# Recommendation tower on one core: embedding features in groups of four instead of three, with both ends of the kernel reordered

## The reference

```python
e = jnp.stack([tbl_0[ids[:, 0]], ..., tbl_26[ids[:, 26]]], axis=1)      # (2048, 27, 128)
inter = einsum('bfd,bgd->bfg', e, e)[:, upper triangle without diagonal]   # 351 pairs
h = concatenate([e.reshape(B, -1), inter, dense_ctx], axis=1)              # dense_ctx: 16 columns
h = maximum(h @ W_top1 + b_top1, 0)    # W_top1 (3823, 512)
h = maximum(h @ W_top2 + b_top2, 0)    # W_top2 (512, 256)
y = h @ W_top3                         # (256, 1)
```

## Time and profile before

| what | before |
|---|---|
| median of 3 runs | 555.32 us (553.8 to 556.41) |
| the profiled execution's own time | 555.27 us |
| its span | 553.3 us |
| mean granted TensorE clock | 0.994 |
| busy: PE, PEld, DVE, ACT, POOL | 515.7, 422.9, 246.4, 256.3, 399.0 us |
| matmuls, gathers | 4337, 411 |

### The profile page before, as it was taken

How to read it: one execution, slowest core, us unless ns; L and a number is a source line. 1 busy time by engine, 2 the same in 40 slices (tenths; PEclk the granted TensorE clock), 3 DMA queues, 4 the chain that set the end, 5 groups by cost and what they waited for, 6 DMA issues and landing times.

```text
span 553.3 us, 12824 instructions
## 1 busy us (share of the span) xinstructions
PE 515.7 (93%) x4337; PEld 422.9 (76%) x4337; DVE 246.4 (45%) x501; ACT 256.3 (46%) x504; POOL 399.0 (72%) x415
## 2 busy tenths in 40 slices
PE   0677999999899999999999998999999999999996
PEld 0556888878688787888788787888878887788884
DVE  3564543535254343635335352443436353362544
ACT  3664545363354545345453533545353453533542
POOL 6777777777777777777777777777777777777700
PEclk9988999999999999999999999999999999999999
DMA  8885222222222222222221222222222222222200
GB/s 178 258 271 171 55 66 55 54 56 55 65 56 51 58 56 65 52 55 55 66 58 50 55 54 64 56 50 56 55 63 53 54 54 64 53 50 54 53 11 2
DMA packets 26553, 38.82 MB, mean 70 GB/s; under 512 B 12510, under 2 KB 16078, under 8 KB 26488
## 3 DMA queue, kind: packets, MB, share of 16 engines
q0 software_dynamic: 13152, 26.96, 18.9%
q1 hardware_dynamic: 10410, 9.95, 6.2%
q10 hardware_dynamic: 2926, 1.09, 0.8%
HBM read 37.96 MB, written 0.01 MB: 69 GB/s over the span
## 4 chain that ended last, share of the span: by engine, by line
PE 61%; POOL 21%; issue 8%; DMA 7%; DVE 2%; ACT 1%; DVEq 0%; ACTq 0%
POOL gathered L331 21%; PE p_hid L712 14%; PE p_hid L714 13%; PE p_hid L713 13%; PE p_prod L784 9%; PE p_group L682 7%; DMA gathered<-tbl_dram,idx 4%; DMA w_stage<-tbl_dram 1%; PE p_group L669 1%; PE p_group L670 1%; PE p_hid_t L749 1%; DVE w_low L495 1%; DMA w_stage<-w_dense_dram 1%; PE p_group L699 1%; ACT emb L380 0%
## 5 line engine op out<-in xcount | busy, mean ns | idle before, releaser
L331 POOL DMA_INDIRECT gathered<-tbl_dram,idx x411 | 398.8, 970 | 127.3 <-issue 119.5
L712 PE MATMUL p_hid<-w_high,emb_high 128*128 128x512 f32 x424 | 180.6, 426 | 0.0
L714 PE MATMUL p_hid<-w_high,emb_low 128*128 128x512 f32 x424 | 168.0, 396 | 0.0
L713 PE MATMUL p_hid<-w_low,emb_high 128*128 128x512 f32 x424 | 166.8, 393 | 0.0
L510 DVE TENSOR_TENSOR emb_low<-p_group,emb_high 128x384 fp32r<-128x384 f32 x144 | 79.1, 549 | 155.9 <-ACT emb L380 155.4
L365 ACT ACTIVATE emb_high<-p_group 128x384 fp32r<-128x384 f32 x144 | 69.9, 485 | 156.2 <-PE p_group L682 139.1
L380 ACT ACTIVATE emb<-p_group 128x384 f32<-128x384 f32 x144 | 124.0, 862 | 0.0
L682 PE MATMUL p_group<-identity,gathered 128*128 128x128 f32 x411 | 72.9, 284 | 29.0 <-DMA gathered<-tbl_dram,idx 28.9
L714 PEld LDWEIGHTS p_hid<-w_high,emb_low 128*128 128x128 f32 x424 | 80.3, 189 | 19.0
L713 PEld LDWEIGHTS p_hid<-w_low,emb_high 128*128 128x128 f32 x424 | 81.1, 191 | 12.6
L712 PEld LDWEIGHTS p_hid<-w_high,emb_high 128*128 128x128 f32 x424 | 81.0, 191 | 12.2
(11 more groups left out here) (86 smaller groups left out, 364.4 us busy)
## 6 DMA issues: line engine op xcount, KB each, us to landing
fetched<-tbl_dram SPq DMA_DIRECT2D x640, 0.5 KB
w_stage<-w_dense_dram SPq DMA_DIRECT2D x27, 256.0 KB, 3.7
gathered<-tbl_dram,idx POOLq DMA_INDIRECT x411
pick_ids<-ids_rows_dram ACTq DMA_DIRECT2D x7, 125.0 KB
w_stage<-w_pairs_dram SPq DMA_DIRECT2D x3, 252.0 KB
w_stage<-w_dram SPq DMA_DIRECT2D x2, 256.0 KB, 4.5
w_stage<-tbl_dram SPq DMA_DIRECT2D x2, 250.0 KB
ctx_sb<-ctx_rows_dram ACTq DMA_DIRECT2D x14, 13.5 KB, 1.8
```

What stands on the lines that cost most here:

```text
L331: pool.indirect_dma_start(gathered[:, slot, k, :], None, tables[f], bass.IndirectOffsetOnAxis(ap=idx[:, t, f:f + 1], axis=0),).then_inc(gr ...
L712: nc.tensor.matmul(dst, high, w_high, start=start, stop=False)
L713: nc.tensor.matmul(dst, high, w_low, start=False, stop=False)
L714: return nc.tensor.matmul(dst, low, w_high, start=False, stop=stop)
```

## The change

1. **Groups of four.** `FEATS = 4`: six groups of four features and one of three in place of nine of three. The order of a tile becomes `[0, 1, 2, 3, 4, 5, "pairs", 6]`, with the rest of the work at the same step numbers; the picks are made at steps 2 and 3.
2. **Rings.** The ring holds 4 groups, 16 gathers; `emb_low` holds two groups in place of three, so `group_low` waits for layer 1 of two groups before.
3. **Start.** SP issues the remaining weights right after the first five, the table of row numbers and the first pick's ids; the ids of tiles 1 to 15 (now laid out so that each partition reads one piece of 1,620 bytes) come after weight piece 8, the context of all tiles (one DMA of 16 columns, in place of one of 27 per tile) after piece 22, the biases and `w3` behind all weights. In tile 0, layer 1 of a group goes ahead of the transposes.
4. **End.** In the last tile, `relu1` and `hid1_to_low` of tile 14 come behind the last group's copies; the four rounds of pair products come behind layer 1 of group 5 and `transpose_hid1`; the bias of the last layer 2 is put in by a matmul (`last_bias2`) in place of DVE's addition.
5. `hid1` shares its memory with `products`; two waits guard it.

```diff
-    FEATS = 3
-    GROUPS = NF // FEATS
-    RING = 6
+    FEATS = 4
+    GROUPS = -(-NF // FEATS)
+    LAST_FEATS = NF - FEATS * (GROUPS - 1)
+    RING = 4
     SPLIT = 3
+    SPLIT_LOW = 2
...
-    SEQUENCE = [0, 1, 2, 3, 4, 5, 6, "pairs", 7, 8]
-    LAST_SEQUENCE = [0, 1, 2, 3, 4, "pairs", 5, 6, 7, 8]
+    SEQUENCE = [0, 1, 2, 3, 4, 5, "pairs", 6]
+    LAST_SEQUENCE = [0, 1, 2, 3, 4, "pairs", 5, 6]
+    PICK_STEPS = [2, 3]
...
+    def feats_of(g):
+        return range(FEATS if g < GROUPS - 1 else LAST_FEATS)
...
-            sp.dma_start(idx[:, 1:TILES, :], ids_t[:, 1:TILES, :]).then_inc(ids_loaded[1], 16)
+            sp.dma_start(table_row_sb[:], table_row).then_inc(table_row_loaded, 16)
+            sp.dma_start(pick_ids_first[:], picked_t[0].partition_broadcast(PICK_ROWS)).then_inc(pick_ids_loaded, 16)
+            for n in range(STAGES, len(STAGED)):
+                load_weight(n)
+                if n == 8:
+                    sp.dma_start(idx[:, 1:TILES, :], ids[:, 1:TILES, :]).then_inc(ids_loaded[1], 16)
+                if n == 22:
+                    sp.dma_start(ctx_sb[:], ctx_rows).then_inc(ctx_loaded, 16)
...
-                    if (ahead_t, ahead) == (LAST, GROUPS - 2):
-                        relu1(LAST - 1)
...
+                if n == GROUPS - 2 and t == LAST:
+                    relu1(LAST - 1)
...
+                wait(dve, group_used, s - SPLIT_LOW + 1)
-                nc.vector.tensor_tensor(emb_low[:, s % SPLIT, 0:n, :], bank_of(t, g)[:, 0:n, :],
+                nc.vector.tensor_tensor(emb_low[:, s % SPLIT_LOW, 0:n, :], bank_of(t, g)[:, 0:n, :],
...
+                wait(dve, hid1_low_done, t)
...
-                nc.vector.tensor_tensor(hid2[:], p_hid2[:, 0:HID2], b2_rows[:], ALU.add).then_inc(bias2_done, 1)
-                dve.wait_ge(bias2_done, t + 1)
-                nc.vector.scalar_tensor_tensor(out=hid2[:], in0=hid2[:], scalar=0.0, in1=w3_rows[:],
+                summed = p_hid2[:, 0:HID2] if t == LAST else hid2[:]
+                if t < LAST:
+                    nc.vector.tensor_tensor(hid2[:], p_hid2[:, 0:HID2], b2_rows[:], ALU.add).then_inc(bias2_done, 1)
+                    dve.wait_ge(bias2_done, t + 1)
+                nc.vector.scalar_tensor_tensor(out=hid2[:], in0=summed, scalar=0.0, in1=w3_rows[:],
...
+            def last_bias2(t):
+                pe.wait_ge(bias2_done, t)
+                nc.tensor.matmul(p_hid2[:, 0:HID2], identity[:], b2_rows[:], start=True, stop=False)
...
+                    if t == 0:
+                        layer1_group(t, n)
                     ahead_t, ahead = ORDER[ORDER.index((t, n)) + 2]
...
-                    else:
+                    elif t > 0:
                         layer1_group(t, n)
...
                 transpose_group(t, 6)
                 layer1_group(t, 5)
                 transpose_hid1(t - 1)
-                transpose_group(t, 7)
-                layer1_group(t, 6)
-                transpose_group(t, 8)
                 for r in range(ROUNDS):
                     pair_products(t, r)
                 layer2(t - 1)
-                layer1_group(t, 7)
-                layer1_group(t, 8, [0])
+                layer1_group(t, 6, [0])
                 last_transpose_pairs(t, [0])
-                layer1_group(t, 8, [1, 2])
+                layer1_group(t, 6, [1, 2])
                 last_transpose_pairs(t, [1, 2])
                 layer1_pairs(t, by_chunk=True)
+                last_bias2(t)
                 last_transpose_hid1(t)
```

More of the change, by code:

```diff
@@ L35, in dlrm_tower @@
     HID2 = w2.shape[1]
-    TILES = B // P
-    CTX = ctx_rows.shape[1]
-    assert D == P and B % P == 0 and TILES % 2 == 0 and TILES >= 6 and NF == 27
+    CTX = ctx_rows.shape[2]
+    assert ids.shape[0] == P and D == P and TILES % 2 == 0 and TILES >= 6 and NF == 27
     assert HID1 == 512 and HID2 <= 512 and HID1 % P == 0
@@ L42, in dlrm_tower @@
     ROWS_I = NF // 3
-    assert CTX == NF
+    assert CTX <= NF
     ROW = DELTAS + 1
@@ L83, in gathered_feats @@
             return range(FEATS)
-        return [k for k in range(FEATS) if g * FEATS + k != PICKED
+        return [k for k in range(LAST_FEATS) if g * FEATS + k != PICKED
                 and not (g * FEATS + k == FETCHED and t in FETCH_TILES)]
-    ids_t = ids.rearrange("(t p) f -> p t f", p=P)
-    ctx_t = ctx_rows.rearrange("(t p) n -> p t n", p=P)
     out_t = out.rearrange("(t p) o -> t (p o)", p=P)
@@ L140, in dlrm_tower @@
         prod = sb("prod", [P, NF, ROWS_Q])
+        with nc.sbuf_tensor("hid1", [P, HID1], F32) as hid1:
+            pass
         products = sb("products", [P, WIDE, ROWS_Q])
@@ L164, in dlrm_tower @@
         group_gathered = [sem(f"group_gathered_{k}") for k in range(RING)]
-        ctx_loaded = [sem(f"ctx_loaded_{k}") for k in range(2)]
+        ctx_loaded = sem("ctx_loaded")
         pick_ids_loaded = sem("pick_ids_loaded")
@@ L308, in _ @@
             sp.dma_start(w3_rows[:], w3.partition_broadcast(P)).then_inc(consts_loaded, 16)
-            for n in range(STAGES, len(STAGED)):
-                load_weight(n)
             sp.wait_ge(fetch_ids_loaded, 16)
@@ L384, in group_copies @@
                 if t == 0:
-                    for n in range(staged_upto(FEATS * g), staged_upto(FEATS * (g + 1))):
+                    for n in range(staged_upto(FEATS * g), staged_upto(FEATS * g + len(feats_of(g)))):
                         weight_high(n)
@@ L410, in last_place_ctx @@
                 act.wait_ge(pairs_transposed, t)
-                act.wait_ge(ctx_loaded[t % 2], (t // 2 + 1) * 16)
-                nc.scalar.activation(pairs[:, :, DELTAS], ctx_sb[:, t % 2, :], ACT.Copy).then_inc(last_placed, 1)
+                act.wait_ge(ctx_loaded, 16)
+                nc.scalar.activation(pairs[:, 0:CTX, DELTAS], ctx_sb[:, t, :], ACT.Copy).then_inc(last_placed, 1)
             def last_place_pairs(t):
@@ L461, in _ @@
                         group_copies(ahead_t, ahead)
-                if n == 0 and t == 0:
+                if n == 0 and t == 2:
                     act.wait_ge(consts_loaded, CONSTS * 16)
@@ L614, in _ @@
                     ahead_t, ahead = ORDER[k + 2]
-                    if (ahead_t, ahead) == (LAST, GROUPS - 3):
+                    if (ahead_t, ahead) == (LAST, GROUPS - 1):
                         copy_hid1(LAST - 1)
-                    if (ahead_t, ahead) == (LAST, GROUPS - 1):
-                        hid1_to_low(LAST - 1)
                     if ahead == "pairs":
@@ L628, in _ @@
                     hid1_to_low(t - 2)
+                if n == GROUPS - 2 and t == LAST:
+                    hid1_to_low(LAST - 1)
                 if n == 4 and t >= 2:
                     layer3(t - 2)
-                if n in (4, 5) and picks_start(t):
-                    make_pick(t, n - 4)
+                if n in PICK_STEPS and picks_start(t):
+                    make_pick(t, PICK_STEPS.index(n))
                 if n == "pairs" and t < LAST:
@@ L685, in transpose_group @@
                     pe.wait_ge(rows_fetched[n % 2], (n // 2 + 1) * P * 16)
-                    last = nc.tensor.transpose(bank_of(t, g)[:, FETCHED % FEATS, :], fetched[:, n % 2, :], identity[:])
+                    last = nc.tensor.transpose(bank_of(t, g)[:, FETCHED - g * FEATS, :], fetched[:, n % 2, :], identity[:])
                 last.then_inc(group_transposed, 1)
```

58 lines of the change are left out of this document (29 added, 29 removed).

## The result

The changed kernel takes 556.52 us (median of 13 runs, 555.71 to 557.7), the kernel before 554.43 us beside it (median of 13, 552.02 to 556.41). The ratio is 1.0037, with a 95% interval of 1.0021 to 1.0053: slower, by 2.1 us, but within the 0.5% that the text called no change. The forecast was +0.9%. The 13 runs of each kernel spread over 4.4 us (before) and 2.0 us (after).

What follows compares the result with a forecast made beforehand. Gathers were taken to pace PE until its last hold, PE's own work after it: span 553.3 + 3.8 (later hold) + 1.3 (end) = 558.4, as a time 560.3 us, +0.9%; own range 558 to 562, 8 in 10 555.5 to 563.

Steps and rivals of the forecast that it cites:

- signs that were to prove the sum wrong: A last gather near 521, or PE past group 5 of tile 14 before 492.
- The kernel's bound: Whole kernel: time is the last hold of PE by a gather, plus PE's work from there.
- PE's prices, hand-over 0: PE: transpose 0.11 us, a feature's layer 1 0.70, product round 1.22, layer 2 1.41, picks 1.91; changing groups costs nothing.
- The hold moves to group 5 of tile 14; no hold in tile 15: PE waits for feature 23, starts those transposes at 493.5, reaches the last group at 536.1, 3.8 us later than before.
- Ring, `emb_low`, ACT's and DVE's chain: 0.0: Shallower buffers and longer copy chains cost 0.0: at least 6 us of ring slack, nearly 2 us to spare in the chain.
- The end: +1.3: From the last group's transposes to the end: 22.3 us against 21.0 before, including a 1.7 us PE wait for pairs.
- The start: 0: New order of weights and ids: bound 0 to -3.8 us, taken as 0, as the same weights land in the same stretch.
- POOL's pace: Gathers one each 1.25 us: feature 23 issued at 490.5, first gather 2.85, last near 525.6.
- The first rival: The start relieves POOL by all 3.8 us (556.5), or the tile 14 hold isn't reached (556.6); chance 0.20.
- faster, by POOL: New ids layout and missing context DMAs take away all 9.0 us the gathers lost: 551.3; chance 0.07.
- Theory C: Theory of the follow-ups: POOL's pace varies by chance between executions and kernels; the term of the groups is as computed.

Runs made afterwards that it cites:

- `tail_after`: Changed kernel with the last tile's layer 1 split, so PE has two features more to do before wanting the first pairs: 554.92 us, ratio 1.0005.
- `new_start`: Kernel before with only the change's start (SP's order, layout of ids, one context DMA, memory shared by `hid1`): 553.68 us, ratio 0.9992.
- `old_start`: Changed kernel with the old order and layout of the ids put back: 556.12 us, ratio 1.0038.
- `short_pick_before`: Kernel before with one-hot operands of tiles 3 to 15 made for 4 of 128 columns, picks incomplete: 552.12 us, ratio 0.9963.
- `short_pick_after`: Changed kernel with one-hot operands of tiles 3 to 15 made for 4 of 128 columns, picks incomplete: 555.73 us, ratio 1.0023.
- `fetch7`: Feature 25 fetched by SP in seven tiles, not five; slow sets: on the changed kernel 758.68 us, ratio 1.0705, on the kernel before 712.02 us, 1.0213.

## Why the prediction was wrong

The direction was right and the size was more than twice too large: +5.0 us on the median against +2.1. The measured 556.5 lies in the range given for 8 in 10 (555.5 to 563), but under the forecast's own 558 to 562. One of the signs that were to prove the sum wrong came true: PE was past group 5 of tile 14 before 492 (its transposes began at 491.03 and take 0.44). By its own steps:

- **The kernel's bound** (last hold of PE plus PE's work): right, in every kernel of the table.
- **PE's prices, hand-over 0**: right. Hold to last group 42.3, in the sum 42.6.
- **The hold moves to group 5 of tile 14; no hold in tile 15**: right in place. The landing took 2.71 us (488.32 to 491.03), in the sum 2.96: 0.25 of the error. It is no chance: 2.6 to 2.7 in all six kernels of groups of four, 3.0 to 3.1 in the three of groups of three.
- **Ring, `emb_low`, ACT's and DVE's chain: 0.0**: right here (POOL's waits for PE at most 0.3 us); it doesn't hold in the three slow sets, where single hand-overs are slower than every row of the trace had shown.
- **The end: +1.3**: right. 22.2 against 22.3, with the wait before the first pair transposes that was put at 1.7 (1.7 on the weight loads, 1.24 on the matmuls), the bias matmul hidden at 548.43. `tail_after` gets 1.2 of it back.
- **The start: 0**: right as an effect of the edit, by `new_start` and `old_start`. The Trainium skill's rule on 512 bytes was right in that the rate rose without the small pieces, and would have been wrong on the time.
- **The step that failed is POOL's pace**: "Feature 23 is 18 gathers behind the one of 468.03, at 490.5", and "first gather 2.85, last near 525.6". The sum carried the 9.0 us that the gathers of the profiled execution had lost against an even 1.25 over into the changed kernel, without knowing what they are. It put 3.8 of them down to the full DMA engines, and said of the other 5.2 only what they are not. They are gathers that began while DVE ran a blocking operation: 10.0 of the 10.8 us of stretches of that trace lie beside two-operand operations of DVE, 0.2 beside the copy into `pairs`. Ahead of that gather (it is the same, the 384th, in both kernels, and in the kernel before it was issued at 490.51) the stretches are 9.4 us before and 7.1 after. It is issued at 488.32: 2.2 us of the error.

Together 2.2 + 0.25 + 0.3 + 0.1 = 2.8 us (rounded), 558.4 - 2.8 = 555.6, the span measured. That the sum started from one profile that lay 0.8 us above the median of 13 runs (555.27 against 554.43) is balanced by the profile after, which lies 0.9 above its own.

The first rival named the right time, 556.5, by luck, for the wrong reason: the hold was reached, and the start relieved nobody. The rival on the fast side, "faster, by POOL", had the right object, the 9.0 us, and named the wrong cause (ids and context DMAs).

With the picks' stretches taken out of both, `short_pick_before` and `short_pick_after` differ by 3.6 us in the medians and 4.5 in the spans; 5.1 was computed, and 0.45 of the 4.5 is that POOL happens to be later (last gathers at 520.18 and 520.63). So by this pair the groups of four and the end cost 3.6 to 4.5 us, near the 5.1 of the sum, and in the profiles the change looked cheaper, because its DVE operations met its gathers less often (7.1 us ahead of the hold against 9.4). That the medians follow the profiles in this is not shown: each kernel has one profile, and 35 runs of the kernel before range from 550.8 to 557.6 us.

**What stays open.** Why the changed kernel's phases fall better isn't shown: both kernels have 14 picks of the same length, and no run moved a pick without shortening it. Theory C is thus half right: with a mechanism, it is still chance for whoever predicts, some 4 us between the profiles of kernels that differ in details. How much the stretches vary between executions of one kernel isn't known. Of the kernels run, only `short_pick_before` is clearly faster than the kernel before, and it leaves work out. Picks with one operand in PSUM, or issued right behind the start of a gather, weren't tried.

## What to carry to other kernels

When a queue paces a kernel, split its losses against the undisturbed period before summing anything: each lost tenth has a row beside it that names its cause, and an unexplained loss is a term of the range, not a constant. Look for DVE operations that read both operands from SBUF, and for long copies within SBUF, beside POOL's indirect DMAs, and make them short: what a gather loses is what such an operation still has to run when the gather begins. Larger groups in a ring of few slots cost the gathers that must have landed at once, and can cost more where hand-overs are slow.

## What was unexpected in the hardware

- A DVE operation with two operands in SBUF that began more than 0.03 us before a gather stretches it by its remaining time less 0.12 to 0.13 us (0.24 for 0.37 left, 0.37 for 0.50, 1.04 for 1.16), in 203 of 203 cases; a copy within SBUF did the same (0.26 for 0.39). One that begins 0.03 us after the gather doesn't, and isn't held up by the gather either (1.22 us).
- With no 108-byte pieces of ids in the stretch from 5 to 12 us the DMA engines moved 287 (`new_start`) and 299 GB/s (after), with them 214, and the gathers ran at the same pace.
- In three of five sets the kernel before took 702 to 710 us, 27 to 28% above the others' 554.4; in the trace of `old_start` there single waits for signals last up to 10.5 us in the row shown. By the ratios of the tables, the kernels with groups of four take 5 to 8% more there than those with groups of three (`old_start` to `new_start` 1.0959 to 1.0175, `fetch7` 1.0705 to 1.0213, short picks 1.1025 to 1.0196), in the other sets 0.5 to 0.6% more (1.0038 to 0.9992, 1.0023 to 0.9963).
